# Building the tensor product with the features already on partitions

## The reference, cut to what matters

```python
x_dst = h[edge_dst]                                   # [E, 64], one gathered row for each edge
wk, wv = mlp2(edge_attr_64, ...), mlp2(edge_attr_64, ...)   # [E, 128] each
# tensor_product(x_e, sh, w, C), sh = edge_attr_9 [E, 9], C [64, 9, 128]:
acc = sh[:, 0:1] * (x_e @ C[:, 0, :])
for s in range(1, 9):
    acc = acc + sh[:, s:s + 1] * (x_e @ C[:, s, :])
k, v = acc_k * wk, acc_v * wv
attn = sum over each head of q[edge_src] * k          # then a softmax over the edges of one node
upd  = segment_sum(v * alpha)                         # [N, 128]
out  = h @ W_self + upd @ W_out                       # then a batch norm, and the residual
```

## Time and profile before

| | |
|---|---|
| time, median of 3 | 3731.14 us |
| the profiled execution | 3729.88 us, its span 3728.2 us |
| layer 0 loop | about 180 to 1238 us |
| middle block | 1242 to 1405 us |
| layer 1 loop | 1406 to 3590 us, one step every 10.67 us |
| last block | 3592 us to the end |
| busy over the span | PE 89%, DVE 77%, POOL 55%, ACT 34% |

### The profile page before, as it was taken

The page is one execution under the profiler, slowest core; times in us unless marked ns, Lnnn a source line. Parts: engine busy times, 40 slices in busy tenths (PEclk is TensorE's granted clock), DMA queues, the critical chain, the costliest instruction groups (busy, mean ns, idle before and its releaser), DMA issues. The chain is left out here.

```text
span 3728.2 us, 86642 instructions
## 1 busy us (share of the span) xinstructions
PE 3330.0 (89%) x25947; PEld 3178.9 (85%) x25947; DVE 2877.5 (77%) x5292; ACT 1285.0 (34%) x3333; POOL 2055.4 (55%) x1999
## 2 busy tenths in 40 slices
PE   2099999999999337999999999999999999999963
PEld 1088888888888237999999999999999999999953
DVE  4366666666666227999999999999999999999943
ACT  1033333333333113444444444444444444444420
POOL 2577777777777435555555555555555555555540
PEclk9599999999999658999999999999999999999975
DMA  8399999999999313444444444444444444444420
GB/s 339 86 268 280 279 279 279 279 280 279 279 280 279 105 46 105 127 126 132 131 124 129 131 129 124 130 132 126 125 132 132 124 128 131 130 124 129 132 78 29
DMA packets 843789, 622.16 MB, mean 167 GB/s; under 512 B 490431, under 2 KB 732803, under 8 KB 843452
## 3 DMA queue, kind: packets, MB, share of 16 engines
q1 hardware_dynamic: 667110, 500.09, 44.2%
q0 software_dynamic: 56640, 87.65, 9.7%
q10 hardware_dynamic: 119982, 33.79, 4.1%
HBM read 335.87 MB, written 286.31 MB: 167 GB/s over the span
## 5 line engine op out<-in xcount | busy, mean ns | idle before, releaser
L1305 POOL DMA_INDIRECT xg<-h_tab,src_i x808 | 861.5, 1066 | 220.8 <-issue 127.2
L789 POOL DMA_INDIRECT kv<-kv_tab,src_i x808 | 762.1, 943 | 285.7 <-issue 188.2
L1315 POOL TENSOR_TENSOR kq<-kvs,q_of 128x512 f32<-128x512 f32 x202 | 260.6, 1290 | 837.7 <-DVE kvs L1491 837.7
L1401 ACT ACTIVATE z_hi<-bank 128x512 fp32r<-128x512 f32 x808 | 439.4, 595 | 802.9 <-PE bank L1333 802.9
L1357 PE MATMUL bank<-C_hi,z_hi 128*128 128x256 f32 x4040 | 682.2, 299 | 0.0
L1357 PE MATMUL bank<-C_lo,z_hi 128*128 128x256 f32 x4040 | 612.2, 281 | 0.0
L1481 DVE TENSOR_TENSOR z_lo<-bank,z_hi 128x512 fp32r<-128x512 f32 x808 | 520.5, 686 | 113.5 <-ACT z_hi L1401 113.4
L1357 PEld LDWEIGHTS bank<-C_hi,z_hi 128*128 128x128 f32 x4040 | 537.8, 191 | 0.3
L1357 PEld LDWEIGHTS bank<-C_lo,z_hi 128*128 128x128 f32 x4040 | 535.3, 188 | 0.0
L1357 PE MATMUL bank<-C_hi,z_lo 128*128 128x256 f32 x3232 | 516.2, 281 | 0.0
L913 DVE TENSOR_TENSOR wsb<-bank,b 128x512 f32<-128x512 f32 x404 | 279.3, 691 | 298.7 <-PE bank L977 298.3
(11 more groups left out here) (248 smaller groups left out, 4754.4 us busy)
## 6 DMA issues: line engine op xcount, KB each, us to landing
w_tab<-wsb SPq DMA_DIRECT2D x202, 512.0 KB, 3.4
win<-w_tab SPq DMA_DIRECT2D x202, 512.0 KB, 3.6
sum_edge<-rowt SPq DMA_DIRECT2D x202, 288.0 KB, 2.5
q_edge<-zq SPq DMA_DIRECT2D x202, 256.0 KB
qs<-q_edge SPq DMA_DIRECT2D x202, 256.0 KB, 2.8
sum_edge<-rows ACTq DMA_DIRECT2D x202, 136.0 KB
qs<-q_edge SPq DMA_DIRECT2D x202, 128.0 KB
drow<-dst_tab SPq DMA_DIRECT2D x202, 128.0 KB, 3.2
```

What stands on the lines that cost most here:

```text
L789: pool.indirect_dma_start(kv[b][:, q, :], None, kv0_tab, bass.IndirectOffsetOnAxis(ap=src_i[:, i * Q + q:i * Q + q + 1], axis=0))\
L1305: pool.indirect_dma_start(xg[b][:, q, :], None, h1_tab, bass.IndirectOffsetOnAxis(ap=src_i[:, i * Q + q:i * Q + q + 1], axis=0))\
L1315: pool.tensor_tensor(kq[:, :].rearrange("p (q o) -> p q o", q=Q), kvs[b][:, :, 0:O1], q_of[b % 2][:, :].rearrange("p (q o) -> p q o", q=Q) ...
L1401: nc.scalar.activation(z_hi[b % 2][:, k, :], bank[ZB[k]][:, :], ACT.Copy).then_inc(hi_out, 1)
```

## The change

z is no longer built with edges on partitions and turned. Instead x is turned (2 transposes for each super-tile), copied by ACT to both 64-partition halves (`xT`), and DVE multiplies it, features on partitions, with the spherical values, which come by DMA repeated over 64 partitions: partitions 0 to 63 hold the even values of s, 64 to 127 the odd ones. For this the middle block writes the values in another order to two tables in DRAM, `sh_tab` and `sh_last_tab`. The ninth part is made straight from the PSUM bank of the turned x. The rounding and the subtraction work on 128x1024 blocks in SBUF. The same-destination matrix moves from DVE to ACT, as relu(1 - (dst_e - drow)^2) in five instructions. q's spread gets a PSUM bank of its own.

Middle block (the program's `SG` is 101; `TAIL` is 213):

```diff
+            SG = NST // 2
+            sh_rows = [sb(f"sh_rows{g}", [SG, ST, S], F32, ph) for g in range(2)]
+            sh_parts = sb("sh_parts", [SG, S, ST], F32, ph)
 # SP
+                    flag = sp.value_load(unsorted[0:1, 0:1])
+                    def load_sh_rows(a):
+                        last_full = (NST - 1) * ST
+                        sp.dma_start(sh_rows[0][:, :, :], a[0:SG * ST, :].rearrange("(p e) s -> p e s", p=SG))...
+                        sp.dma_start(sh_rows[1][0:NST - 1 - SG, :, :],
+                                     a[SG * ST:last_full, :].rearrange("(p e) s -> p e s", e=ST))...
+                        sp.dma_start(sh_rows[1][NST - 1 - SG:NST - SG, 0:TAIL, :], a[last_full:E, :].unsqueeze(0))...
                     load_last_rows(sp, lrows, sum0_edge, last_got)
+                    sp.wait_ge(sh_padded, 1)
+                    (load_sh_rows of the values as given, or as ordered)
 ...                 (zeros into carry1_tab; wait for c_put; load car)
+                    for g in range(2):
+                        sp.wait_ge(sh_parts_set, g + 1)
+                        sp.dma_start(sh_tab[g * SG:(g + 1) * SG], sh_parts[:, 0:S - 1, :]).then_inc(sh_put, 16)
+                        sp.dma_start(sh_last_tab[g * SG:(g + 1) * SG, :], sh_parts[:, S - 1, :]).then_inc(sh_put, 16)
                     sp.wait_ge(h1_ready, 1)
 ...
+                    sp.wait_ge(sh_put, 64)
 # ACT, after the copies of crows and before those of wvT
+                    act.wait_ge(sh_rows_in, 48)
+                    for g in range(2):
+                        if g:
+                            act.wait_ge(sh_put, 32)
+                        for r in range(2):
+                            nc.scalar.activation(sh_parts[:, 4 * r:4 * r + 4, :],
+                                                 sh_rows[g][:, :, r:S - 1:2].rearrange("p e c -> p c e"), ACT.Copy)
+                        for r in range(2):
+                            ins = nc.scalar.activation(... sh_parts[:, S - 1, half r] ..., of_half(sh_rows[g][:, :, S - 1], r), ACT.Copy)
+                        ins.then_inc(sh_parts_set, 1)
 # DVE, first
+                    dve.memset(sh_rows[1][96:SG, TAIL:ST, :], 0.0).then_inc(sh_padded, 1)
```

Layer 1 loop:

```diff
 # SP
-                        load_either(sp, sh_turn, flag, i, sh[b][:, :, :], ea9, ea9_s, sh_in[b], sh_tail)
+                        need(sp, z_last_ready, i - 1)
+                        for f, e in zip(rows_of, edges_of):
+                            sp.dma_start(sh_last[b % 2][f, :], sh_last_tab[bass.ds(i, 1), e].broadcast_to([D, ST // 2]))...
+                        need(sp, z_ready, i * 2 - 2)
+                        for r, f in enumerate(rows_of):
+                            sp.dma_start(sh[b % 2][f, :, :]..., sh_tab[bass.ds(i, 1), 4 * r:4 * r + 4, :]
+                                         .rearrange("a c e -> a (c e)").broadcast_to([D, 4 * ST]))...
 # POOL
-                    unrolled([(times_q, -1), (gather_x, 4)], RING)
+                    unrolled([(times_q, -1), (gather_x, 5)], RING)
 # PE
-                    def t_z(k): ...
+                    def turn_x(it, i, b):
+                        pe.wait_ge(x_got[b], 16 * Q * (it + 1))
+                        need(pe, x_out, i - 1)
+                        need(pe, z_last_ready, i - 1)
+                        for h in range(Q // 2):
+                            ins = nc.tensor.transpose(bank[b % 2][:, h * P:(h + 1) * P], xg[b][:, 2 * h:2 * h + 2, :]..., ident[:, :])
+                        ins.then_inc(x_mm, 1)
+                    pipelined(pe, [(turn_x, 3), (turn_max, -2), (sums, -3), (m_acc(0), 0), (m_acc(1), 0), (turn_logits, -1),
+                                   (spread_q, 0), (m_acc(2), 0), (m_acc(3), 0)], RING)
 # ACT
+                    def take_x(it, i, b):        # four copies of 64x256, PSUM to both halves of xT
+                    def hi(k):                   # k = 0, 1: 128x1024 from z to z_hi; waits z_ready
+                    def hi_last(it, i, b):       # two copies of 64x256 from z_last
+                    def apart(it, i, b):         # after drow: four Squares of 128x128 with a bias from dst_e
+                    def build(it, i, b):         # one Relu of 128x512 on the same tile, bias 1, scale -1
+                    pipelined(act, [(hi(0), 1), (copy_max, -2), (weights, -2), (take_x, 3), (take_sums, -3), (hi(1), 1),
+                                    (apart, 1), (hi_last, 1), (take_q, 0), (build, 1)], RING)
 # DVE
+                    def outer(k):
+                            dve.wait_ge(x_out, i + 1)
+                            dve.wait_ge(sh_in[b % 2], 64 * (2 * it + b // 2 + 1))
+                            need(dve, lo_out, i * 3 - 5 + k)
+                            c = slice(2 * k, 2 * k + 2)
+                            dve.tensor_tensor(z[b % 2][:, c, :], bcast(xT[b % 2][:, :], 1, 2), sh[b % 2][:, c, :], ALU.mult)...
+                    def outer_last(it, i, b):
+                        dve.tensor_tensor(z_last[b % 2][:, :], bank[b % 2][:, 0:2 * P], sh_last[b % 2][:, :], ALU.mult)...
+                    def lo(k):                   # k = 0, 1: z_lo = z - z_hi, 128x1024, all in SBUF
+                    def lo_last(it, i, b):       # two subtractions of 64x256, all in SBUF
-                    def build(it, i, b): ...
+                    pipelined(dve, [(product(1), -1), (subtract, -2), (outer(0), 2), (logits, -1), (weigh, -2), (lo(0), 1),
+                                    (outer_last, 2), (lo(1), 1), (outer(1), 2), (lo_last, 1), (segment_max, -1),
+                                    (product(0), 0)], RING)
```

More of the change, by code:

```diff
@@ L1365, in turn_logits @@
                         pe.wait_ge(attn_ready, i + 1)
[L1367 to L1371, removed]
+                        need(pe, max_copied, i)
                         nc.tensor.transpose(bank[SHARED][0:Q * H1, 0:P], attn[b % 2][:, :], ident[:, :]).then_inc(attn_mm, 1)
@@ L1393, in _ @@
                 @block.scalar
                 def _(act):
+                    def take_x(it, i, b):
+                        act.wait_ge(x_mm, i + 1)
+                        need(act, z_ready, i * 2 - 2)
+                        for f in rows_of:
+                            for r, g in enumerate(rows_of):
+                                ins = nc.scalar.activation(of_half(xT[b % 2][f, :], r),
+                                                           bank[b % 2][g, 0:2 * P].rearrange("p (h e) -> p h e", e=P), ACT.Copy)
+                        ins.then_inc(x_out, 1)
@@ new lines, in apart @@
+                    def apart(it, i, b):
+                        act.wait_ge(drow_in[b % 2], 16 * (2 * it + b // 2 + 1))
+                        need(act, sum_mm, i - RING + 1)
+                        for q in range(Q):
+                            ins = nc.scalar.activation(same[b][:, q, :], drow[b % 2][:, q * P:(q + 1) * P], ACT.Square,
+                                                       bias=dst_e[:, bass.ds(i * Q + q, 1)], scale=-1.0)
+                        ins.then_inc(apart_ready, 1)
@@ L1409, in take_q @@
+                    def build(it, i, b):
+                        act.wait_ge(apart_ready, i + 1)
+                        nc.scalar.activation(same[b][:, :, :], same[b][:, :, :], ACT.Relu, bias=one[:, :], scale=-1.0)\
+                                 .then_inc(same_ready, 1)
+                    act.wait_ge(max_zero, 2)
                     def take_q(it, i, b):
@@ L1481, in stage @@
[L1481 removed]
+                            c = slice(2 * k, 2 * k + 2)
+                            dve.tensor_tensor(z_lo[b % 2][:, c, :], z[b % 2][:, c, :], z_hi[b % 2][:, c, :].bitcast(F32),
                                               ALU.subtract).then_inc(lo_out, 1)
                         return stage
+                    def lo_last(it, i, b):
+                        dve.wait_ge(hi_out, i * 3 + 3)
+                        need(dve, a_mm, i * 2 - 2)
+                        for r in range(2):
+                            f, g = rows_of[r], rows_of[1 - r]
+                            ins = dve.tensor_tensor(of_half(z_hi[b % 2][g, 4, :], r),
+                                                    z_last[b % 2][f, :].rearrange("p (h e) -> p h e", e=P),
+                                                    of_half(z_hi[b % 2][f, 4, :], r).bitcast(F32), ALU.subtract)
+                        ins.then_inc(lo_out, 1)
```

152 lines of the change are left out of this document (68 added, 84 removed).

## The result

The changed kernel takes 3827.8 us (median of 4 runs, 3816.2 to 3839.5) against 3731.6 for the kernel before on the same chip: 1.026 times as long, interval 1.0225 to 1.0289. Forecast were 3852 us, slower. The profiled execution took 3816.15 us, its span is 3814.4, 86.2 more than the span before. Ratios and intervals compare only runs within 1.5% of the fastest of their kernel, and in experiments 5 and 8 these are two of four, without the profiled one, though the granted clock was the same in all four to 0.003.

A forecast was written before the change was run, and what follows sets the result against it. PE was taken to set the 10.67 us step, DVE 6% behind. 3729.9 + 130 (middle block) + 5 (loop's start) - 14 (loop) = 3851, as a median 3852 us; own range 3795 to 3930.

The forecast's parts named there:

- The middle block: Between the layer loops: slower loads and stores of the values shift everything behind by 130 us, bounds 100 to 160.
- one engine for 101 rows: Middle block: a 101-row transfer runs on one DMA engine at 26 GB/s, 71.6 us for 1.86 MB.
- ACT's copies of one group: Middle block: ACT copies 4608 columns of one group of values in 4.3 us.
- zeros and `car`: Middle block: these transfers, late through the shared DMA engine, end at 1352, ahead of the first group's store.
- DVE's list: Layer 1 loop: DVE's own operations sum to 9.15 us a step.
- The lock: Layer 1 loop: POOL's multiply and outer(0) cannot run together, so logits waits; adds 1.4 us to the step.
- rival 1: Layer 1 loop: the multiply runs beside outer(0), step 9.35 to 9.9 us, total 3600 to 3710 us; chance 0.22.
- The added traffic: Layer 1 loop: load_sh's extra 1.18 MB a step takes 4.2 us of all DMA engines, hidden under 10.6.
- Rival 4: Layer 1 loop: the repeated loads bound the step at 11 or 12 us, total 3930 to 4130 us; chance 0.06.
- ACT: Layer 1 loop: with its added work ACT takes 7.9 to 8.3 us of a step, hidden.
- PE: Layer 1 loop: sixteen transposes go, PE's list falls from 10.67 to 8.95 us a step; no clock drop expected.
- The loop's start: Layer 1 loop's start: the first m_acc stands behind the fourth super-tile's gather instead of the third's, +5 us.

The follow-up runs named there:

- Experiment 5: kernel 1 with POOL's multiply cut in two halves and outer_last moved ahead of outer(0): 3629.9 to 3719.5 us, 0.977 of the kernel before.
- experiment 8: Experiment 5's kernel with the sh load of the upper 64 partitions issued by ACT instead of SP: 3604.4 to 3689.8 us, 0.968 of the kernel before.
- experiment 9: Experiment 5's kernel with the two 64-row sh loads made one of 128 rows, source sizes 2, 64, 2048: 6630.0 us.
- experiment 3: experiment 2's kernel with the sh loads bringing half their bytes, both outer multiplies reading the same half (wrong values): 3612.9 us, step 9.39 us.
- experiment 6: experiment 2's kernel with the two 64-row sh loads made one of 128 rows from one DRAM row (wrong values): 3618.3 us, step 9.39 us.
- experiment 2: The changed kernel with outer(0) taking x from PSUM instead of the SBUF copy (wrong values): 3873.3 us, step 10.66 us.
- experiment 4: The changed kernel with the same-destination matrix made on DVE again and ACT's five instructions for it gone: 3937.1 us, step 10.98 us.
- kernel 7: experiment 2's kernel with each sh load reading 64 different rows instead of one row 64 times (wrong values): 3844.5 us, step 10.52 us.
- kernel 1: The changed kernel with each 101- or 100-row transfer cut into 96 rows and the rest: 3695.1 us, 0.991 of the kernel before.

## Why the prediction was right

**The middle block, +130 forecast, +132 measured** at `wvT` (1431.97 for 1299.85), +133.9 at the loop's start. The step that nothing of before showed, one engine for 101 rows, was taken from the 125-row load and held: the first strided copy stood at 1332 in the sum and started at 1332.43; `q_tab` was to be issued at 1496 and was at 1496.90. The rule in the Trainium skill ("DMA: Bandwidth & Descriptors", Why a DMA increments its semaphore by 16 and not by 1) gives the same, and this case's traces agree in three sizes: 125, 101, and the 2 of experiment 9.

**Two terms inside it were mis-sized.** ACT's copies of one group were put at 4.3 us and took 8.6 (1332.43 to 1341.07): 7.54 us for 2 x 2048 columns are 1.84 ns a column where it reads every ninth value; 0.85 came from reads in a row out of PSUM, and `hi`, in a row out of SBUF, takes 1.06 us for 1024 columns, 1.04 each. The sum also put 16 us of zeros and `car` between the copies and the store, slow by the shared engine. SP stood still earlier instead, 23 us in the issue of the second load and 62 in that of the zeros. Both were over by 1339.15, and the store was issued at 1341.09, right behind the copies. ACT's wait from there was 82 us for 74. That the second group began at 1423.4, against 1425 in the sum, is luck: 4 us too little for the copies and 7 too much for the rest nearly cancel.

**DVE's list, 9.15 forecast.** From `logits` to the next `product(0)` the sum was 6.68 and the trace has 6.72. A subtraction of 128x1024, bounded at 1.09 and 1.25, is 1.22 long.

**The lock, +1.4 forecast, 1.2 measured.** `logits` starts 3.1 us after `product(1)` (2508.22, less 2505.13) where I had 3.3. The multiply ended 1.16 after `outer(0)` and not 1.30, and `outer(0)` began 0.69 after `product(1)`, where the sum counted from 0.75. The sum of 10.55 plus 0.05 for waits became 10.42, and these 0.18 us are 36 of the 38.5 us between -14 and -52.5 in the loop. The gathers of the earlier trace rows had shown the same lock, and experiment 3 shows it for a multiply: 2.31 and 1.29. Experiment 5 shows the other order, which the prediction had named ("whichever goes first"). The rule of the Trainium skill ("SBUF — State Buffer", Who interferes with whom) is borne out by these numbers. The sum of rival 1, the step without the lock, was good too: 9.35, and 9.39 in experiments 3 and 6. Only its condition didn't hold.

**The added traffic, 4.2 us forecast, 5.4 measured.** The share of 0.98 times 10.42 is 10.2, less 4.8, if the old traffic costs what it did. Without that condition, the 8 KB packets of `sh` alone, 1.05 MB, take 570 ns each or 4.6 us of all engines. This was the weakest term: 283 GB/s was taken from a stage of mixed traffic, and the 64-row loads got 1.18 MB / 5.4 us = 220. With 128 rows (experiment 6) it is 0.87 x 9.39 - 4.8 = 3.4 us, 350 GB/s (packets of `sh` 2.9 us). The forecast's "hides under 10.6" held, with a share of 0.98 and nothing to spare, and "less well under 9.35" is what experiment 2 ran into. Rival 4 had a chance of 0.06; as the bound of this kernel it was wrong (experiment 4), as the bound right behind it right, and it deserved more. The Trainium skill ("SBUF — State Buffer", Door 1), which lets 64 partitions reach half the ports, put this load at 6.0 us, an estimate from its 196 GB/s: nearer to 5.4 than my 4.2.

**ACT** was busy 368.9 of 500 us, 7.7 of a step (7.9 to 8.3 forecast), and nothing but the usual waits showed: hidden. **PE** was idle 12% at clock 1.00, with 9.1 us of work in a step (8.95 forecast). **The loop's start** cost 7.7 for 5.

The total came out 24 us under the forecast: +4 in the middle, +3 at the start, -38 in the loop, -3 at the end make -34 for the profiled execution, which was the fastest of the four.

Open stays why kernels 2 and 7, bound by the loads, run slower (10.66 and 10.52) than the changed kernel at 10.39 with the same bytes. In them the rate wanders from window to window (226 to 246 GB/s in kernel 2), while it stands at 242 to 244 where the lock paces the loop. The same wandering is in kernels 5 (225 to 252) and 8 (224 to 255), whose four runs spread by 90 and 85 us, against 23 and 18 for the changed kernel and kernel 1. That late loads collide with the gathers would fit; it was not tried.

## What to carry to other kernels

Before rows are dealt out to a DMA, look at the outermost size of both sides: 96 + 5 rows instead of 101 was worth 133 us here, more than the whole change of the loop. A gain in an engine's list is worth only the distance to the next bound, and that next bound must be priced in DMA time with its own shape (partitions written, outermost size), not by bytes. And when DVE work is moved so that POOL's SBUF work falls under an operation with two SBUF inputs, the two times add, whichever starts first.

## What was not expected of the hardware

- Behind long loads the issuing engine stands too: nine DMAs of zeros took SP 61.67 us to issue with the loads on one DMA engine, 29.62 with them spread, and 9.31 without them.
- 1.18 MB by loads to 64 partitions cost 5.4 us of all engines; the same bytes with 1.05 MB of them to 128 partitions 3.4. A packet of 8 KB took 570 ns in the first, 361 in the second.
- A source with outermost size 2 ran on two engines although it wrote 128 rows: a step of 24.7 us.
- ACT reads values 36 bytes apart in SBUF at 1.84 ns a column, against 1.04 for adjacent ones.
